# Decoder layer with a gated recurrence: input and forget gates projected by channel, rescaled by a broadcast row

## What is computed

```
def _bitlinear(x, w):                  # ternary weights, 8-bit tokens
    xn = _rmsnorm(x)
    s = 127.0 / clip(max(abs(xn), axis=-1, keepdims=True), 1e-05)
    xq = clip(round(xn * s), -128, 127) / s
    ws = 1.0 / clip(mean(abs(w)), 1e-05)
    wq = clip(round(w * ws), -1, 1) / ws
    return einsum('bld,od->blo', xq, wq)

i = silu(_bitlinear(x, Wi)) * (1.0 - f)        # f = sigmoid(_bitlinear(x, Wf))
h = scan over the 512 tokens of a batch: h[t] = f[t] * h[t-1] + i[t]
o = _rmsnorm(_bitlinear(x, Wg)) * g_norm_weight * (h * sigmoid(h))
x = _layernorm(x + _bitlinear(o, Wo))
```

## Time and profile before

| | us |
|---|---|
| median of 3 runs | 393.69 |
| lowest and highest | 390.56 and 394.14 |
| span of the profiled execution (first to last instruction) | 391.8 |
| attention part, to the start of the expert part on PE | 178.7 |
| expert part | 213.1 |

### The profile page before, as it was taken

How to read it: one execution, slowest core, us unless ns; L and a number is a source line. 1 busy time by engine, 2 the same in 40 slices (tenths; PEclk the granted TensorE clock), 3 DMA queues, 4 the chain that set the end, 5 groups by cost and what they waited for, 6 DMA issues and landing times.

```text
span 391.8 us, 6465 instructions
## 1 busy us (share of the span) xinstructions
PE 307.0 (78%) x1531; PEld 220.0 (56%) x1541; DVE 260.9 (67%) x654; ACT 199.4 (51%) x359; POOL 184.8 (47%) x297
## 2 busy tenths in 40 slices
PE   1165867486777769837788999999999999999870
PEld 0124344243434334415557888888888888888650
DVE  4899897488979786822545666666666666665641
ACT  3776977385666767313334444444444444444330
POOL 0338875575655574621123344444444444443342
PEclk9999899988969898995999999999999999999986
DMA  7995377657272643113001111111111111100000
GB/s 243 383 386 209 66 150 141 96 148 186 53 185 43 172 72 90 54 56 108 0 2 46 22 58 52 59 32 54 54 54 54 59 53 65 60 31 28 28 28 6
DMA packets 17735, 36.10 MB, mean 92 GB/s; under 512 B 2286, under 2 KB 2542, under 8 KB 17712
## 3 DMA queue, kind: packets, MB, share of 16 engines
q0 software_dynamic: 7056, 16.53, 17.7%
q1 hardware_dynamic: 10656, 19.31, 14.4%
HBM read 26.64 MB, written 11.02 MB: 96 GB/s over the span
## 4 chain that ended last, share of the span: by engine, by line
PE 46%; DVE 2%; issue 2%; ACT 2%; POOL 2%; DVEq 0%; POOLq 0%
PE bank L1209 13%; PE bank L1213 13%; PE bank L1210 12%; PE bank L1201 6%; PE bank L1224 2%; POOL d L1035 1%; DVE st L1126 1%; ACT rows L1104 0%; ACT x L1099 0%; DVE mv L1132 0%; POOL v L1033 0%; POOL out L1049 0%; DVE b L1137 0%; DVE r L1163 0%; ACT x L1092 0%
## 5 line engine op out<-in xcount | busy, mean ns | idle before, releaser
L1033 POOL TENSOR_TENSOR v<-mv,eps_c 128x1 f32<-128x1 f32 x57 | 11.6, 203 | 112.7 <-DVE mv L1132 112.4
L873 PE MATMUL bank<-w_q,xq_t 128*128 128x512 bf16 x191 | 52.2, 434 | 6.0 <-issue 5.3
L1144 DVE TENSOR_TENSOR hid<-bank,act_z 128x512 f32<-128x512 f32 x19 | 13.1, 691 | 42.8 <-ACT act_z L1081 42.8
L873 PEld LDWEIGHTS bank<-w_q,xq_t 128*128 128x128 bf16 x192 | 21.0, 112 | 34.6 <-issue 17.0
L1074 ACT ACTIVATE h_hi<-bank 128x512 fp32r<-128x512 f32 x19 | 11.4, 599 | 46.2 <-PE bank L1201 46.2
L1035 POOL TENSOR_TENSOR d<-v,minus_half 128x1 f32<-128x1 f32 x57 | 32.4, 568 | 4.5
L1209 PE MATMUL bank<-f_hi,m_hi 128*128 128x512 f32 x76 | 32.0, 421 | 0.7 <-ACT m_hi L1074 0.7
L1092 ACT ACTIVATE x<-r,b,d 128x512 f32<-128x512 f32 x19 | 15.5, 816 | 32.4 <-DVE b L1137 32.4
L1209 PE MATMUL bank<-c_hi,h_hi 128*128 x76 | 31.5, 415 | 0.3 <-issue 0.2
L1209 PE MATMUL bank<-c_hi,a_hi 128*128 x76 | 30.2, 397 | 1.0 <-ACT a_hi L1074 0.8
L1210 PE MATMUL bank<-f_lo,m_hi 128*128 128x512 f32 x76 | 30.7, 404 | 0.0
(11 more groups left out here) (155 smaller groups left out, 832.7 us busy)
## 6 DMA issues: line engine op xcount, KB each, us to landing
f_sum<-in_factors POOLq DMA_DIRECT2D x7, 1024.0 KB, 9.3
rows<-sorted_rows SPq DMA_DIRECT2D x19, 256.5 KB, 2.6
c_stage<-in_ctx_t SPq DMA_DIRECT2D x8, 512.0 KB, 6.2
xs<-in_x SPq DMA_DIRECT2D x1, 3072.0 KB, 18.9
w_stage<-in_wi_t SPq DMA_DIRECT2D x1, 1024.0 KB, 5.9
xs<-in_x SPq DMA_DIRECT2D x2, 512.0 KB, 8.8
w_stage<-in_wf_t SPq DMA_DIRECT2D x1, 1024.0 KB, 8.4
w_stage<-in_wg_t SPq DMA_DIRECT2D x1, 1024.0 KB, 10.5
```

Of the source, the lines that this page charges most:

```text
L873: last = t.matmul(bank[:], xq_t[:, j, c, :], w_q[:, m, c, :], start=(c == 0), stop=(c == KC - 1))
```

## The change

The input and forget gates are projected with the weights as the stationary and the quantised tokens as the moving operand, so the result has channels on the partitions: 4 groups of 4 matmuls of 256 columns for each gate. The factor x_mc of a token then lies along the free axis. PE spreads it over the partitions by two transposes of a broadcast column (spread_max), ACT copies that row to SBUF (max_row), and DVE multiplies each projection by it on the way from PSUM to SBUF (rescale_f, rescale_i: four instructions per turn). Silu and tanh then work in place in SBUF with w_deq as scale. The sixteen float32 transposes per turn are gone; gate_i and the scans read SBUF only. Both gates go through the same two banks, so the i projection waits for rescale_f. The g matrix is projected as before, by token, but after both gates.

```diff
+        b_ch = (b_i, b_f)
+        b_mc = b_i[:, 0:GW]
@@ ACT
+                def max_row(g, half):
+                    act.wait_ge(s.tmc, g + 1)
+                    after(act, s.di, 2 * (g - 1))
+                    nc.scalar.activation(mc_row[:, half, :], b_mc, ACT.Copy).then_inc(s.mcb, 1)
-                    nc.scalar.activation(i_tok[:, j, :], b_i[:], ACT.Silu, scale=deq[:, half, 0, j:j + 1]
-                    nc.scalar.activation(t_tok[:, j, :], b_f[:], ACT.Tanh, scale=deq[:, half, 1, j:j + 1]
+                def silu_i(g, c):
+                    act.wait_ge(s.di, 2 * g + c + 1)
+                    i = i_ch[:, c, :, :].rearrange("p a n -> p (a n)")
+                    nc.scalar.activation(i, i, ACT.Silu, scale=w_deq[:, 0:1]).then_inc(s.silu, 1)
+                def tanh_f(g, c):
+                    act.wait_ge(s.df, 2 * g + c + 1)
...
@@ ACT turn
                     if have(0):
-                        silu_i(g, half, 0)
+                        tanh_f(g, 0)
                         if first:
                             weight_sum(3)
                     if have(-1):
                         square_o(p, 1)
                     if have(0):
-                        tanh_f(g, half, 0)
+                        tanh_f(g, 1)
+                        forget(g, 0)
+                        silu_i(g, 0)
                         square_g(g, 0)
-                        silu_i(g, half, 1)
-                        tanh_f(g, half, 1)
+                        silu_i(g, 1)
                         square_g(g, 1)
-                        forget(g, 0)
                         forget(g, 1)
...
                         x_by_channel(g + 1, 1)
+                        max_row(g + 1, 1 - half)
@@ DVE
+                def rescale(g, half, c, dst, s_z, s_done):
+                    dve.wait_ge(s_z, 2 * g + c + 1)
+                    dve.wait_ge(s.mcb, g + 1)
+                    v.tensor_tensor(dst[:, c, :, :], b_ch[c][:].rearrange("p (a n) -> p a n", a=PC),
+                                    mc_row[:, half, None, :].to_broadcast([P, PC, GW]), ALU.mult).then_inc(s_done, 1)
...
-                        v.tensor_tensor_scan(h_ch[:, half, c, a, :], f_ch[:, c, a, :], b_ti[c][:, a * GW:(a + 1) * GW],
+                        v.tensor_tensor_scan(h_ch[:, half, c, a, :], f_ch[:, c, a, :], i_ch[:, c, a, :],
@@ DVE turn
                         output(p, 1)
+                    if have(0):
+                        rescale_f(g, half, 0)
+                        rescale_f(g, half, 1)
+                    if have(-1):
                         o_max_of(p, 0)
                         o_max_of(p, 1)
                     if have(1):
                         x_max_normed(g + 1)
+                    if have(0):
+                        rescale_i(g, half, 0)
+                        rescale_i(g, half, 1)
                     if have(-1):
                         o_mean_square(p)
@@ PE
+                def spread_max(g):
+                    pe.wait_ge(s.xmc, g + 1)
+                    after(pe, s.di, 2 * (g - 1) + 1)
+                    for j in range(GT):
+                        last = t.transpose(b_mc[:, j * P:(j + 1) * P], x_mc[:, j:j + 1].to_broadcast([P, P]), k.ident[:])
+                    last.then_inc(s.tmc, 1)
+                def project_channels(g, m, c, s_free, free, s_done):
+                    pe.wait_ge(s.xq, tile(g, GT))
+                    after(pe, s_free, free)
+                    weights_here(g, m)
+                    for a in range(PC):
+                        ch = (PC * c + a) * P
+                        for i in range(KC):
+                            last = t.matmul(b_ch[c][:, a * GW:(a + 1) * GW], w_q[:, m, i, ch:ch + P], xq_t[:, :, i, :],
+                                            start=(i == 0), stop=(i == KC - 1))
+                    last.then_inc(s_done, 1)
+                def project_tokens(g, j):
...
+                def project(g):
+                    pe.wait_ge(s.mcb, g + 1)
+                    for c in range(2):
+                        project_channels(g, 1, c, s.di, 2 * (g - 1) + c + 1, s.zf)
+                    for c in range(2):
+                        project_channels(g, 0, c, s.df, 2 * g + c + 1, s.zi)
@@ PE turn
                     if have(0):
-                        project(g, 0)
+                        project(g)
                         if isinstance(g, int) and g == 0:
                             weight_total(3)
-                        project(g, 1)
-                    if have(0):
-
-                        for c in range(2):
...
-                            by_channel(t_tok, b_tt[c], c, s.tt)
+                        project_tokens(g, 0)
+                        project_tokens(g, 1)
                     if have(1):
                         transpose_x(g + 1, 0)
                         transpose_x(g + 1, 1)
+                        spread_max(g + 1)
...
-                            by_channel(i_tok, b_ti[c], c, s.ti)
```

More of the change, by code:

```diff
@@ L131, in attention @@
         xq_t = sb("xq_t", [P, GT, KC, P], BF16)
-        i_tok = sb("i_tok", [P, GT, D])
-        t_tok = sb("t_tok", [P, GT, D])
+        i_ch = sb("i_ch", [P, 2, PC, GW])
+        t_ch = sb("t_ch", [P, 2, PC, GW])
+        mc_row = sb("mc_row", [P, HALVES, GW])
         gated = sb("gated", [P, GT, D])
@@ L172, in attention @@
             sqx mxx xve xr xmr xmc xrc xq_s deq q tx xq zi zf zg silu tanh sqg gg ii
-            gt1 gt2 gve gr gf tt ti fe scan sh tsh o mxo sqo ot1 ot2 ove o_r ofr omf omr omc orc oq_s oa
-            qo to eo wo r number place hi split route rmm
+            gt1 gt2 gve gr gf fe scan sh tsh o mxo sqo ot1 ot2 ove o_r ofr omf omr omc orc oq_s oa
+            qo to eo wo r number df di tmc mcb place hi split route rmm
             scat0 scat1 hold_pool hold_act hold_dve""", lambda n: sem("a_" + n))
@@ L406, in _ @@
                     x_by_channel(0, j)
+                max_row(0, 0)
                 weight_ready(1)
                 weight_ready(2)
[L410 to L414, removed]
-                    nc.scalar.activation(i_tok[:, j, :], b_i[:], ACT.Silu, scale=deq[:, half, 0, j:j + 1]
[L416 to L421, removed]
-                    nc.scalar.activation(t_tok[:, j, :], b_f[:], ACT.Tanh, scale=deq[:, half, 1, j:j + 1]
-                                         ).then_inc(s.tanh, 1)
+                def silu_i(g, c):
[4 more added lines that the diff above has]
+                    act.wait_ge(s.df, 2 * g + c + 1)
+                    f = t_ch[:, c, :, :].rearrange("p a n -> p (a n)")
+                    nc.scalar.activation(f, f, ACT.Tanh, scale=w_deq[:, 1:2]).then_inc(s.tanh, 1)
                 def square_g(g, j):
@@ L452, in forget @@
                 def forget(g, c):
-                    act.wait_ge(s.tt, 2 * g + c + 1)
+                    act.wait_ge(s.tanh, 2 * g + c + 1)
                     after(act, s.scan, 4 * (g - 1) + 2 * c + 2)
-                    nc.scalar.activation(f_ch[:, c, :, :].rearrange("p a n -> p (a n)"), b_tt[c][:], ACT.Copy,
+                    nc.scalar.activation(f_ch[:, c, :, :].rearrange("p a n -> p (a n)"),
+                                         t_ch[:, c, :, :].rearrange("p a n -> p (a n)"), ACT.Copy,
                                          bias=0.5, scale=0.5).then_inc(s.fe, 1)
@@ L555, in x_max_guarded @@
                     dve.wait_ge(s.xmr, g + 1)
+                    after(dve, s.tmc, g)
                     v.tensor_scalar(x_mc[:], x_mr[:], GUARD, None, ALU.max).then_inc(s.xmc, 1)
@@ L564, in x_rescales @@
                     dve.wait_ge(s.xmc, g + 1)
-                    after(dve, s.tanh, tile(g - 1, 0))
                     after(dve, s.gf, g - 1)
@@ L581, in quantise_x, with rescale_f, rescale_i, gate_i @@
                                     x_q[:, j:j + 1], HALF_MAGIC, ALU.mult, ALU.add).then_inc(s.q, 1)
[L583 to L587, removed]
+                def rescale(g, half, c, dst, s_z, s_done):
[3 more added lines that the diff above has]
+                                    mc_row[:, half, None, :].to_broadcast([P, PC, GW]), ALU.mult).then_inc(s_done, 1)
+                def rescale_f(g, half, c):
+                    after(dve, s.fe, 2 * (g - 1) + c + 1)
+                    after(dve, s.ii, 2 * (g - 1) + c + 1)
+                    rescale(g, half, c, t_ch, s.zf, s.df)
+                def rescale_i(g, half, c):
+                    after(dve, s.scan, 4 * (g - 1) + 2 * c + 2)
+                    rescale(g, half, c, i_ch, s.zi, s.di)
+                def gate_i(g, c):
+                    dve.wait_ge(s.tanh, 2 * g + c + 1)
+                    dve.wait_ge(s.silu, 2 * g + c + 1)
+                    i, f = (a[:, c, :, :].rearrange("p a n -> p (a n)") for a in (i_ch, t_ch))
+                    v.scalar_tensor_tensor(i, f, 1.0, i, ALU.subtract, ALU.mult).then_inc(s.ii, 1)
                 def weigh_g(g, j):
@@ L858, in transpose_x, with weights_here @@
                     transpose_halves(b_q[j], xq, j, s.tx)
```

(14 more changed lines are left out.)

4 lines of the change are left out of this document (1 added, 3 removed).

## The result

The changed kernel takes 411.01 us (median of 4 runs, 409.74 to 412.07), the kernel before 393.26 beside it (4 runs): a ratio of 1.047, 95% interval 1.044 to 1.050. The profiled execution took 412.07 with a span of 410.4; before it was 391.8. So the span grew by 18.6 us; by the medians the growth is 17.7.

A forecast was written before the change was run, and what follows sets the result against it. The prediction took the chain through DVE, held by POOL's c_lo, as the bound, not PE. Growth by turns summed to 18.6 us, taking the span from 391.8 to 410.4 and the median to 412 us; main-case range 405 to 418.

The forecast's parts named there:

- The bound: Turn 5 chain through DVE: the next T is o_q plus 5.97 us (end of c_lo) plus 3.46 us (scans, silu_h).
- For turn 2 the 0: Turn 2 grows by 0, since g_f on DVE stood idle 5.23 us for the factor's DMA and 2 us fit in.
- Turn 5, step by step after T: Engine steps from T(5): weigh_g starts at 9.4 or 9.5 us instead of 7.28, and the turn grows by 2.3.
- The mis-sized term for turn 3: Turn 3 starts late with PE idle, then at low clock; i and g projections wait, so it grows by 3.5 us.
- Rival (a): DVE's waits swallow the rescales in turns 3 to 6, weigh_g no later than now; 400 us, chance 0.11.
- What comes: Four DVE instructions of 128 x 512 a turn: 2.5 us a turn, 20 us over eight turns, if nothing hides it.
- Scans and c_lo: Scans with two SBUF operands meet POOL's c_lo in turns 1, 6 and 7; up to 3.0 us, taken as 0 to 1.5.
- the forecast for turn 6: Turn 6 grows by 2.3 us, with a span of -0.5 to +2.4 by who wins the scans.
- The rule weighed ahead: VectorE with two SBUF inputs and GpSimd reading SBUF lock each other out; every new scan exposed, no rescale.
- Turn 0 and the experts: Turn 0 grows by 3.3 us as four rescales and ACT's chain delay its scans; turn 8 and the expert part 0.
- (b): PE at low clock through a turn's projections, or weight loads not hidden: weigh_g 4.2 us late, 422 us, chance 0.11.
- (c): Faster: DVE's held small instruction and scans get ahead of c_lo in turns 3 to 6; 391, down to 386 us, chance 0.05.

The follow-up runs named there:

- before_plus4: The kernel before with four spare DVE multiplications of PSUM by an SBUF row per turn in turns 1 to 7; 397.15 us, ratio 1.008.
- after_low_late: The changed kernel with POOL's c_lo moved from before the normalisation of g to behind that of the next x; 393.30 us, ratio 1.003.
- no_rescale: The changed kernel without the multiplication by x_mc (all four rescales), ACT reading the projections in PSUM; 408.70 us, ratio 1.039.
- scan_psum: The changed kernel with gate_i writing the gate to PSUM, from where the scans read it; 407.96 us, ratio 1.040.

## Why the prediction was right, and where only by its sum

- **The size.** 18.6 us of span predicted, 18.6 measured; 412.0 for 411.01. The terms are off by up to 1.1 us each way and cancel, which is luck. That the spans agree to 0.1 is luck as well: the profiled execution was the slowest of four.
- **The bound.** T(g + 1) is o_q plus the end of c_lo plus 3.46: held. In turns 4 and 5 o_q to the next T is the same to 0.02 us; L675 lasts 3.35 as L655 did. For turn 2 the 0 was right and its reason wrong: the wait for the factor's DMA lies behind T(3), and what took the delay in was the wait for o_r (1.21 us) and the transposes' 0.53, which the prediction had found in turn 6 alone.
- **Turn 5, step by step after T.** Rescales of f end at 4.5 and 5.4 (4.2 and 5.9 predicted), o_max at 6.5 (7.1), rescales of i at 7.8 (8.5), ACT's chain at 8.55 (9.4), weigh_g at 8.58 (9.4). The order is right and the term is too large by 0.8, as the clock was back before T + 4 (0.65 over 122.71 to 124.71, then 1.00) and not at 6.2. The prediction had said that it starts as low since PE is idle as long or longer; PE was idle less, 3.25 us for 4.05. The mis-sized term for turn 3 has the same sign (2.6 for 3.5).
- **The cause inside the term.** "DVE's work 9.1, ACT's chain 9.4" had both, and the runs show how much that pair weighs. Rival (a), waits that swallow the rescales, was rejected because g is projected later; `before_plus4` shows that rejection right for the reason given: the waits do swallow them (1.008) if g stays where it was. So the 2.5 us a turn by which the part "What comes" opens can't be charged as such: removing all four rescales gave 3 of 17.7 us.
- **Scans and c_lo.** The exposure was foreseen for turns 1, 6 and 7, and the forecast for turn 6 mis-sized: 3.0 for 2.3, 0.6 of it behind o_q. Over the kernel the second SBUF operand is worth 2.5 us. The rule weighed ahead (the Trainium skill, SBUF — State Buffer, Who interferes with whom) held for the scans: one with two SBUF inputs lasted 3.98 us, two with one input 1.25 together. The prediction told it too widely: that section spares an instruction with one SBUF input only outside the modes that use both ports, and names tensor_scalar among those that can enter them. L551 of the last section is a tensor_scalar; no run shows which mode it ran in.
- **Turn 0 and the experts.** The scans of turn 0 end at 40.61, as forecast (40.7), which makes 4.1 at T(1) where 3.3 was booked; the first output of turn 1 was late by 2.3 only (43.54 for 41.24), so turn 1 took part of it back. The 1.1 at the end were put at 0 and are not explained; 0.9 of them lie before the expert part starts on PE.
- **Rivals.** (b), the low clock through the projections, didn't come. (c) didn't come as put: L675 is held as long as before. Its lower end was also added wrongly: 391 less twice 1.53 is 388, not 386. But its core, that the path hangs on where c_lo stands, is what `after_low_late` showed: with it moved, the change costs nothing.

## What to carry to other kernels

Before you price added work on the engine that sets the pace, list its waits in that stretch and what releases them: here 17.9 us of it cost 3, while a producer moved to the end of another engine's order cost the turn nearly the same with the work and without it. When two chains end within 0.1 us of each other, undoing one shows little, as `no_rescale` did; undo both, or shift one and look for the wait that appears. And try the order of the engine that nobody is waiting for by name: one POOL step moved gave back 17.7 us of the changed kernel, and the same step split in two, one half earlier and one later, gave 4 in the kernel before.

## What the runs showed of the hardware that I had not expected

An instruction of 128 x 2 with one SBUF input was held by c_lo as well, in turn 3 of the changed kernel, where its shortest execution takes 0.16 us:

```profile
77.33 3.12 DVE L551 TENSOR_SCALAR x_ve<-x_ss 128x2 f32<-128x2 f32 x1
77.45 2.97 POOL L296 TENSOR_TENSOR c_lo<-c_stage,c_hi 128x512 f32 x2
```

The prediction had read one SBUF input as safe. The hold cost the turn nothing, as g_f behind it had to wait for POOL's g_r until 81.39 anyway. By the records the instruction that starts first doesn't win either: L551 starts 0.12 us ahead of c_lo, L681 of `scan_psum` 0.25 and this scan of turn 6, with c_lo at 155.28, 0.41, and each lasted until both of POOL's instructions were over:

```profile
154.87 3.98 DVE L695 TENSOR_TENSOR_SCAN h_ch<-f_ch,i_ch 128x256 f32<-128x256 f32 x1
```

This doesn't settle who was first: in all three cases c_lo's record begins 0.4 to 0.5 us before the one of POOL's DMA issue (L307) ends, so its start is known no better than that. This overlap, and not DVE, also goes with a pair of 3.0 us: one took 2.97 at 72.78 of the kernel before while DVE stood idle, and one took 2.49 at 54.92 of the changed kernel, with no DMA issue right in front, while two scans beside it took 2.47.

The clock can fall inside a turn, too. In the changed kernel it is 0.50 from 134.7 to 136.7, after PE had waited 2.36 us for DVE's xq, and the eight matmuls of project_back take 3.48 us there:

```profile
134.23 3.48 PE L940 MATMUL bank<-w_q,oq_t 128*128 128x512 bf16 x8
```

They end at 137.71, and L675's hold at 137.84, so this costs the turn nothing.
